# ScalarE's own gated functions in place of tanh and a VectorE operation, in the gates of the experts and the last SiLU

## The reference

```python
gate_up = jnp.einsum('th,ehj->etj', h, gate_up_proj) + gate_up_proj_bias[:, None, :]
gate = jnp.minimum(gate_up[..., ::2], LIMIT)
up = jnp.clip(gate_up[..., 1::2], -LIMIT, LIMIT)
glu = gate * jax.nn.sigmoid(gate * ALPHA)           # ALPHA = 1.702
act = (up + 1.0) * glu
expert_out = jnp.einsum('eti,eih->eth', act, down_proj) + down_proj_bias[:, None, :]
...
s = attention(xn)
g = _silu(ffn(xn))                                  # z * sigmoid(z)
x = x + s * g
```

## Time and profile before

| what | value |
|---|---|
| median of 3 runs | 1091.36 us (1091.31 to 1091.75) |
| the profiled execution: its own time | 1086.14 us |
| its span, first to last instruction | 1084.4 us |
| PE busy | 932.2 us (86%) |
| DVE busy | 938.8 us (87%) |
| ACT busy | 769.4 us (71%) |
| POOL busy | 284.1 us (26%) |

### The profile page before, as it was taken

The page is one execution under the profiler, slowest core; times in us unless marked ns, Lnnn a source line. Parts: engine busy times, 40 slices in busy tenths (PEclk is TensorE's granted clock), DMA queues, the critical chain, the costliest instruction groups (busy, mean ns, idle before and its releaser), DMA issues. The chain is left out here.

```text
span 1084.4 us, 25051 instructions
## 1 busy us (share of the span) xinstructions
PE 932.2 (86%) x6626; PEld 652.0 (60%) x6627; DVE 938.8 (87%) x1857; ACT 769.4 (71%) x1982; POOL 284.1 (26%) x478
## 2 busy tenths in 40 slices
PE   4999968898988999898989898987999999993665
PEld 3877745666666666666666666664565556552444
DVE  6777858999999999999999999993777777775997
ACT  3545437999999999999999999993333333335673
POOL 3000001233333333331000000023666666651000
PEclk9999996999999999999999999998999999996788
DMA  6988966666857586756855564611222222225454
GB/s 220 326 305 288 318 255 132 143 140 142 188 134 153 138 188 143 156 130 129 117 117 123 110 133 99 141 19 39 82 82 83 82 82 82 82 73 170 155 177 132
DMA packets 89630, 157.52 MB, mean 145 GB/s; under 512 B 19613, under 2 KB 48797, under 8 KB 89565
## 3 DMA queue, kind: packets, MB, share of 16 engines
q1 hardware_dynamic: 80544, 137.52, 50.0%
q0 software_dynamic: 9056, 19.67, 5.9%
HBM read 104.66 MB, written 52.49 MB: 145 GB/s over the span
## 5 line engine op out<-in xcount | busy, mean ns | idle before, releaser
L1144 DVE TENSOR_REDUCE nmax<-bank 128x1 f32<-128x1024 f32 (+3 forms) x256 | 260.3, 1017 | 6.6 <-PE bank L976 6.6
L1077 ACT ACTIVATE Pr_long<-bank,nmax 128x1024 f32<-128x1024 f32 (+3 forms) x256 | 251.9, 984 | 9.9 <-DVE nmax L1144 9.8
L1104 ACT COPY AT<-bank 128x512 f32<-128x512 f32 (+3 forms) x384 | 177.0, 493 | 3.8 <-PE bank L1015 1.8
L974 PE MATMUL bank<-Ks_first,Qs_first 128*128 128x512 f32 (+3 forms) x384 | 124.0, 413 | 28.8 <-ACT Pr_short L1091 19.6
L1091 ACT ACTIVATE Pr_short<-bank,nmax 128x128 f32<-128x128 f32 (+3 forms) x256 | 138.3, 540 | 9.4 <-DVE nmax L1162 1.5
L1349 PE MATMUL bank<-gu_sb,xsT 128*128 x288 | 141.0, 613 | 3.0 <-DVE hid L1453 0.5
L1015 PE MATMUL bank<-ident,Pr_long 128*128 128x128 f32 x832 | 127.6, 280 | 18.4 <-DVE Pr_long L1194 18.2
L847 POOL COPY VO<-Ob 128x64 f32 (+1 forms) x128 | 30.3, 237 | 414.7 <-ACT Ob L1113 414.3
L1194 DVE SCALAR_TENSOR_TENSOR Pr_long<-Pr_long,coef 128x1024 f32<-128x1024 f32 (+3 forms) x128 | 137.6, 1075 | 0.0
L974 PE MATMUL bank<-Ks_second,Qs_second 128*128 128x512 f32 (+3 forms) x384 | 119.7, 400 | 20.1 <-ACT Pr_short L1091 19.9
L976 PE MATMUL bank<-maskb,identb 128*128 128x128 bf16 x512 | 117.8, 233 | 0.0
(11 more groups left out here) (162 smaller groups left out, 1692.6 us busy)
## 6 DMA issues: line engine op xcount, KB each, us to landing
q_parts<-PARTS SPq DMA_DIRECT2D x32, 512.0 KB, 3.5
k_parts<-PARTS SPq DMA_DIRECT2D x32, 512.0 KB, 4.4
Qs_first<-q_parts SPq DMA_DIRECT2D x64, 256.0 KB
Ks_first<-k_parts SPq DMA_DIRECT2D x64, 256.0 KB
Qs_second<-q_parts SPq DMA_DIRECT2D x64, 256.0 KB
Ks_second<-k_parts SPq DMA_DIRECT2D x64, 256.0 KB
yg<-y_dram SPq DMA_DIRECT2D x16, 512.0 KB, 5.4
X<-x SPq DMA_DIRECT2D x8, 512.0 KB, 6.0
```

The lines of the kernel that those rows point to most:

```text
L974: nc.tensor.matmul(at[:, c0:c1], Qs[head][:, m, q * P:(q + 1) * P], Ks[head][:, m, c0:c1], start=True, stop=(c1 < N))
L1077: nc.scalar.activation(long_probs(p)[:, m, 0:N], long_slot[m][:, 0:N], ACT.Exp, bias=nmax[:, 4 * p + m:4 * p + m + 1], scale=1.0, accum_ou ...
L1104: nc.scalar.copy(AT[u % 6][:, 0:w], tb[u % BANKS][:, 0:w]).then_inc(unit_out, 1)
L1144: nc.vector.tensor_reduce(nmax[:, 4 * p + m:4 * p + m + 1], long_slot[m][:, 0:N], AX.X, ALU.max, negate=True).then_inc(long_maxed, 1)
```

## The change

Both curves are now evaluated by functions of ScalarE that contain the product. The gate becomes `Gelu_apprx_sigmoid`, x times sigmoid(1.702 x), written into `glu` at once, and the last SiLU becomes `Silu`, written into `ft`. The two VectorE operations that made the product from tanh (old L1472 and L1769) go, with their semaphores; `output` becomes a plain addition, and the gain of the root loses its factor 1/2. In `activate` DVE clips `up` first and then waits for `glu` from ACT. ACT, before it overwrites a `glu`, waits for DVE's product of two tiles before (`act_ready`), where it waited for `glu_ready`.

```diff
-                    nc.scalar.wait_ge(glu_ready, seen(it, u - 2))
-                    nc.scalar.activation(gate_tanh[u][:], hid[u][:, 0:I], ACT.Tanh, scale=ALPHA / 2
-                                         ).then_inc(tanh_ready, 1)
+                    nc.scalar.wait_ge(act_ready, seen(it, u - 2))
+                    nc.scalar.activation(glu[u][:], hid[u][:, 0:I], GLU).then_inc(glu_ready, 1)
...
-                    nc.vector.wait_ge(tanh_ready, seen(it, u))
-                    nc.vector.scalar_tensor_tensor(out=glu[u][:], in0=gate_tanh[u][:], scalar=1.0,
-                                                   in1=hid[u][:, 0:I], op0=ALU.add, op1=ALU.mult
-                                                   ).then_inc(glu_ready, 1)
+                    nc.vector.wait_ge(hid_ready, seen(it, u))
                     nc.vector.tensor_scalar(up[u][:], hid[u][:, I:], LIMIT, -LIMIT, ALU.min, ALU.max
                                             ).then_inc(up_ready, 1)
+                    nc.vector.wait_ge(up_ready, seen(it, u))
                     nc.vector.wait_ge(glu_ready, seen(it, u))
-                    nc.vector.wait_ge(up_ready, seen(it, u))
...
-                    nc.vector.scalar_tensor_tensor(out=ys[u][:], in0=ybank[u][:, 0:D], scalar=0.5,
-                                                   in1=dnb_sb[:, bass.ds(e, 1), :].rearrange("p o n -> p (o n)"),
-                                                   op0=ALU.mult, op1=ALU.add).then_inc(y_ready, 1)
+                    nc.vector.tensor_tensor(ys[u][:], ybank[u][:, 0:D],
+                                            dnb_sb[:, bass.ds(e, 1), :].rearrange("p o n -> p (o n)"), ALU.add
+                                            ).then_inc(y_ready, 1)
...
-                        nc.scalar.activation(root[:], square_sum[:], ACT.Sqrt, scale=1.0 / half_gain ** 2
+                        nc.scalar.activation(root[:], square_sum[:], ACT.Sqrt, scale=1.0 / gain ** 2
                                              ).then_inc(root_ready, 1)
...
-                        nc.scalar.activation(ft[h][:], ff[h][:], ACT.Tanh, scale=0.5).then_inc(ft_ready, 1)
+                        nc.scalar.activation(ft[h][:], ff[h][:], ACT.Silu).then_inc(ft_ready, 1)
...
                         dve.wait_ge(ft_ready, credited(b, 2, h))
-                        nc.vector.scalar_tensor_tensor(out=ft[h][:], in0=ft[h][:], scalar=1.0, in1=ff[h][:],
-                                                       op0=ALU.add, op1=ALU.mult).then_inc(silu_ready, 1)
-                        dve.wait_ge(silu_ready, credited(b, 2, h))
                         for k in range(2):
```

More of the change, by code:

```diff
@@ L14 @@
 AX = mybir.AxisListType
+GLU = ACT.Gelu_apprx_sigmoid
 B, S, D = 4, 1024, 256
@@ L18 @@
 T = B * S
-E, I, LIMIT, ALPHA = 8, 256, 7.0, 1.702
+E, I, LIMIT = 8, 256, 7.0
 L_INIT = 0.8 - 0.6 * math.exp(-0.3 * 1)
@@ L1235, in build @@
             hid = [sb(f"hid{u}", [P, 2 * I], where=ph) for u in range(2)]
-            gate_tanh = [sb(f"gate_tanh{u}", [P, I], where=ph) for u in range(2)]
             glu = [sb(f"glu{u}", [P, I], where=ph) for u in range(2)]
@@ L1247, in build @@
             gate_ready = sem("gate_ready")
-            tanh_ready = sem("tanh_ready")
             glu_ready = sem("glu_ready")
@@ L1432, in _ @@
                 def _(act):
-                    for s in (xsT_ready, tanh_ready, act_T_ready):
+                    for s in (xsT_ready, glu_ready, act_T_ready):
                         act.sem_inc(s, 2)
@@ L1492, in output @@
                     nc.vector.wait_ge(y_stored[u], 16 * (it + 1))
-                    nc.vector.scalar_tensor_tensor(out=ys[u][:], in0=ybank[u][:, 0:D], scalar=0.5,
-                                                   in1=dnb_sb[:, bass.ds(e, 1), :].rearrange("p o n -> p (o n)"),
-                                                   op0=ALU.mult, op1=ALU.add).then_inc(y_ready, 1)
+                    nc.vector.tensor_tensor(ys[u][:], ybank[u][:, 0:D],
+                                            dnb_sb[:, bass.ds(e, 1), :].rearrange("p o n -> p (o n)"), ALU.add
+                                            ).then_inc(y_ready, 1)
                 @block.vector
                 def _(dve):
-                    for s in (hid_ready, gate_ready, glu_ready, up_ready, act_ready, y_ready):
+                    for s in (hid_ready, gate_ready, up_ready, act_ready, y_ready):
                         dve.sem_inc(s, 2)
@@ L1544, in build @@
             ft_ready = sem("ft_ready")
-            silu_ready = sem("silu_ready")
             gated = sem("gated")
@@ L1551, in build @@
             HT = CT // 2
-            half_gain = math.sqrt(GROUP) * (1.0 - L_INIT) / 2
+            gain = math.sqrt(GROUP) * (1.0 - L_INIT)
             with nc.Block(no_gpsimd_drain=True) as block:
@@ L1716, in _ @@
                         dve.sem_inc(s, 4)
-                    for s in (summed, ms_ready, recip_ready, ff_ready, silu_ready, gated, res_ready):
+                    for s in (summed, ms_ready, recip_ready, ff_ready, gated, res_ready):
                         dve.sem_inc(s, 2)
```

## The result

The changed kernel takes 1073.76 us (median of 4 runs, 1071.82 to 1074.39), where the kernel before takes 1091.34 us (4 runs, 1089.14 to 1091.75). The ratio is 0.9844 (95% interval 0.9833 to 0.9856). That is 17.6 us less, where 6.5 us had been forecast and where the range allowed 9.6.

The account below looks back on a forecast made before the run. The prediction took PE to bound the expert stage and DVE the last stage. Its terms, +0.3 - 9.0 + 2.2 = -6.5 us, took 1091.36 to 1084.9 us, with a range of 1081.8 to 1089.0.

Parts of the forecast that it names:

- What bounds the expert stage: Expert-stage loop: PE is the bound, DVE and ACT run beside it with 0.96 us of slack, so 0 us gained.
- The entry: Start of the expert stage: a table load ahead of the first gate costs 0.6 us, between 0 and 1.3.
- drain: Last tiles of the expert stage: PE waits for the chain, so some of the 0.42 us returns, -0.3 us.
- The new functions: ACT's gated curves take as long as the tanh: 0.42 us in the expert stage, 1.06 us in the last.
- that rival: Entry of the expert stage: a switch of table sets costs 1.4 us more, total 1086.3 us; chance 5%.
- The last stage: Eight chunks lose L1769, 9.0 us saved on DVE's chain, less 2.2 us given back by late expert rows.
- the 2.2 forecast: Last stage: late expert rows delay `ff` of c4 and c6, giving back 1.1 us each.
- the first rival: Last stage: loads of c4 and c6 get as fast as c3's, nothing given back, 1082.6 us; chance 20%.
- The end: Last projection after c6: c6's saving passes on to it; TensorE's clock may move the end 1.5 us either way.

Follow-up runs that it names:

- after_late_up: The changed kernel with the clip of `up` moved back behind the wait for `glu`: 1066.99 us, ratio 0.9812 to the kernel before.
- gates_only: The kernel before with only the gates moved to the gated function, the last SiLU still by tanh: 1078.97 us, ratio 0.9889 to the kernel before.
- fill_off: The changed kernel plus one unread DVE operation per tile, sized like the removed one, behind `act_in`: 1069.62 us, ratio 0.9812 to the kernel before.
- before_again: The kernel before, unchanged, measured and profiled a second time: 1089.58 us, ratio 0.999.
- silu_only: The kernel before with only the last SiLU moved to the gated function, the gates still by tanh: 1081.52 us, ratio 0.9907 to the kernel before.
- fill_on: The changed kernel plus one unread DVE operation per tile, sized like the removed one, ahead of `act_in`: 1072.72 us, ratio 0.9845 to the kernel before.
- after_sp: The changed kernel with SP asking for chunk c+3's expert rows before the store of c lands: 1066.52 us, ratio 0.9796 to the kernel before.
- best: The changed kernel with PE's expert-number load ahead of its wait and SP's earlier request for expert rows: 1065.2 us, ratio 0.980 to the kernel before.
- before_up: The kernel before with only DVE's clip of `up` moved ahead of the wait for the tanh: 1076.16 us, ratio 0.9903.

## Why the prediction was wrong

**What bounds the expert stage: the step that failed.** I measured 0.96 us of slack between the end of `act_in` and the matmul that turns it, concluded "All of this lies beside PE: 0 us", and laid 47.5 us of "issue" to pauses within PE's own queue. The slack was taken at the wrong consumer. Who waits for `act_in` is PE's queue, and behind that wait stood the branch, the load of the number and the next `gate_and_up`, of which the array felt only the end: 1.41 us after `act_in`, `gate_and_up` started, with no room at all. The term that failed is this 0 us. The loop's 34 passes at 0.33 us make 11 us, nearly all of the 11.7 between the stage's 241.06 and the 229.38 of after_late_up. The changed kernel's profile shows only 5.8, because irregular passes took 6.2; gates_only measured 12.3 us in the median of its runs. The experiments show the ring as the cause: a shorter way through DVE, or the load taken out of the ring, gives the 6.04 us, and DVE's work put back outside of the ring (fill_off) takes nothing from it.

**The entry.** Forecast +0.6 us, between 0 and 1.3. In the trace of the changed kernel:

```profile
746.82 1.28 ACT L1418 ACT_TABLE_LOAD   x1
751.45 0.42 ACT L1418 ACTIVATE glu<-hid 128x256 f32<-128x256 f32 x1 [3.35 <-DVE hid L1463]
...
751.97 0.43 DVE L1478 SCALAR_TENSOR_TENSOR act_in<-up,glu 128x256 f32<-128x256 f32 x1
...
752.45 0.44 PE L1363 MATMUL bank<-ident,act_in 128*128 128x128 f32 x2 [0.27 <-DVE act_in L1478]
```

The table load ran before the wait for the gate, in time in which ACT was idle, so it cost nothing, and from the curve's start to PE it is 1.00 us instead of 1.66: -0.66. The lower case of my bounds was right, and below it, because I hadn't counted the removed operation there. The **drain** gave back nothing (5.74 us before and 5.73 after from the last `hid` to the last scatter), where I had -0.3. I had taken PE to wait for `act_in` there. In the changed kernel the last `act_in` ends at 971.75, PE turns it at 972.49, and ahead of this stands a `down` that waited 0.93 us for ACT's `act_T`, as it did before.

**The new functions.** 0.42 us for 256 columns and 1.06 us for 1024, as the tanh: right. So was the table load, 1.28 us. In the last stage the root follows 0.01 us behind its load, which starts 0.24 us after ACT's work before it, as soon as the sum of squares is there:

```profile
1004.86 1.28 ACT L1676 ACT_TABLE_LOAD   x1 [0.24 <-DVE square_sum L1732]
1006.15 0.42 ACT L1676 ACTIVATE root<-square_sum 128x256 f32<-128x256 f32 x1
```

By the 1.38 us drain at a switch of sets that the Trainium skill gives in "ScalarE: Activation LUTs", "What ACT_TABLE_LOAD costs", the rows could not read so: neither ahead of the load nor behind it is there room for 1.38 us. In none of the 16 loads of this stage, before or after the change, is there a gap of that size. At the entry the trace can't tell, since ACT waited 3.35 us behind the load anyway; it cost nothing there, and that rival fell.

**The last stage: mechanism right, size 1.6 us off.** Two of its rounds, by the starts of L1772 in c1 to c3, and `ff` of c4 and c6 in the changed kernel:

```profile
1011.16 1.23 DVE L1772 TENSOR_TENSOR xr<-ft,xr 128x1024 f32<-128x1024 f32 x1
...
1021.07 1.23 DVE L1772 TENSOR_TENSOR xr<-ft,xr 128x1024 f32<-128x1024 f32 x1
...
1030.88 1.23 DVE L1772 TENSOR_TENSOR xr<-ft,xr 128x1024 f32<-128x1024 f32 x1
```

```profile
1022.85 1.71 ACT L1667 ACTIVATE ff<-yg,yw 128x256 f32<-128x256 f32 x4 [1.28 <-DMA yg<-y_dram]
...
1043.30 1.70 ACT L1667 ACTIVATE ff<-yg,yw 128x256 f32<-128x256 f32 x4 [1.83 <-DMA yg<-y_dram]
```

A round was 9.91 us where 9.91 was forecast, and `ff` of c4 and c6 are released by the transfer. But c4 was only 0.55 us behind `res_ready` (1021.07 + 1.23 = 1022.30) and gave back 0.13; c6 was 1.29 behind and gave back 0.9 (a round of 10.54 us). That is 1.2 us less than the 2.2 forecast. The other 0.4 us is the round from c5 to c6, which shrank by 1.6 us, from 11.08 to 9.48, where 1.26 was counted. The second load of c4 landed 5.7 us after its issue, where in the first profile before it had taken 6.7:

```profile
DMA to landing us min/median/max: 4.9/5.3/5.7
```

The change needn't be what hurried it: in before_again, the unchanged kernel, this load landed after 5.7 us too. In silu_only, with the same last stage, the loads of c4 took 5.4 to 6.6 us, `ff` of c4 and c6 started 1.45 and 1.53 us after `res_ready`, and the rounds were 9.68, 9.90, 10.71, 9.90, 10.79. There the forecast, a round of 10.8 us and 1.1 given back, was met to a tenth:

```profile
1030.55 1.70 ACT L1670 ACTIVATE ff<-yg,yw 128x256 f32<-128x256 f32 x4 [2.17 <-DMA yg<-y_dram]
```

So the changed kernel stands between my forecast and the first rival (the loads hurry). In fill_on it was c3 as well whose rows came late (6.2 us, a round of 10.40). What makes a load land sooner or later stays open; after_sp shows that the chain of SP was the cause of what was given back, by taking it away.

**The end.** The last projection took 5.24 us (5.40 before) and moved nothing here. Over the kernels it took 3.72 to 6.13 us, and the time from `res_ready` of c6 to the end went with it, from 8.2 us (fill_off, best, after_late_up, each at 3.72) over 9.7 (the changed kernel) to 10.5 (before_again, at 6.13). The 1.5 us either way that I had allowed are about right.

**The range.** It contained nothing for a gain in the expert stage. Its edges came from the last stage and the entry alone, as the bound of PE had been taken for shown. A rival with the question "is something of PE's queue waiting where its array is not?" would have been worth 12 us. (The first rival's time, 1091.36 - 8.7, is 1082.7 and not 1082.6 us.)

## What to carry to other kernels

Slack at a wait is measured against the queue that executes it, not against the array or the first busy row of the engine that follows. What stands behind the wait (branches, register loads, the next stage's first matmul) has its own time to serve, and an engine that the profile calls 99% busy can still be paced by a ring through it (59.31 of 60 us in the middle of the stage). Such a ring hides under "issue". In the trace it shows where the same pair of matmuls stands further apart at the top of the loop (0.44 us) than in the middle of a pass (0.22). What it costs only an experiment told: 6.37 us a pass against 6.04. The cheapest repair is to take the register load out from behind the wait. That gave 11.5 us here in a kernel in which the removal of 72 operations gave 12.3.

## What the hardware showed that I had not expected

PE's load of four registers from the expert list took 0.52 us in some kernels and 0.33 in others (0.42 in fill_on), nearly steadily within each, for the same code. Reordering one operation on DVE was enough to change it (before_up). The second load of c4's expert rows landed after 5.5 to 6.9 us in the kernels with SP's old order, with no cause that I found. And one and the same loop took 229.2 to 235.2 us by irregular passes, which is more than several of the effects studied here: one profile doesn't decide on the last 5 us, and for the changed kernel even the median of four executions lies 3 us from what its parts promise.
